# A graph layer on one core: slot products set between the steps of the edge run

## The reference, cut to what matters

```python
h = jnp.maximum(_layernorm(x, axis=-1), 0.0)
m = h[src] + edge_attr
aggr = jax.ops.segment_sum(m, dst, num_segments=N_NODES)
hidden = jax.nn.relu(aggr @ W1 + b1)
mlp_out = hidden @ W2 + b2
return x + (1.0 + eps[0]) * h + mlp_out
```

## Time and profile before

| | us |
|---|---|
| median of 3 runs (545.75 to 546.79) | 546.37 |
| span of the profiled execution | 559.3 |
| PE busy | 493.2 (88%) |
| DVE busy | 486.6 (87%) |
| ACT busy | 418.4 (75%) |
| POOL busy | 337.2 (60%) |

### The profile page before, as it was taken

One profiled execution on the slowest core, in us unless ns is written; L12 is line 12 of the kernel. 1 busy time (PEld: TensorE's weight loads), 2 busy tenths in 40 slices (PEclk: granted clock), 3 DMA queues, 4 the chain that ended last, 5 costly groups with the idle time before them and its releaser, 6 DMA issues.

```text
span 559.3 us, 23317 instructions
## 1 busy us (share of the span) xinstructions
PE 493.2 (88%) x9560; PEld 462.1 (83%) x9560; DVE 486.6 (87%) x712; ACT 418.4 (75%) x637; POOL 337.2 (60%) x200
## 2 busy tenths in 40 slices
PE   0436899999989999999999899999998999999995
PEld 0325799999878888889999798899887998999994
DVE  7996999999997978898999789899896889999960
ACT  0798778888776867868888578788774788788771
POOL 1310003888888888888888888888888878000000
PEclk9999999999999999999999999999998999999998
DMA  7689988988889979999989789998876779667000
GB/s 193 237 283 279 273 268 263 280 219 222 206 226 244 268 205 249 246 276 228 241 212 235 169 206 259 300 225 235 219 199 154 207 207 239 187 203 214 16 10 19
DMA packets 99110, 120.58 MB, mean 216 GB/s; under 512 B 71160, under 2 KB 72792, under 8 KB 98870
## 3 DMA queue, kind: packets, MB, share of 16 engines
q1 hardware_dynamic: 74854, 108.13, 64.0%
q0 software_dynamic: 24144, 10.89, 15.1%
HBM read 112.50 MB, written 6.48 MB: 213 GB/s over the span
## 4 chain that ended last, share of the span: by engine, by line
PE 78%; ACT 8%; DVE 7%; issue 5%; DMA 1%; SPq 0%; DVEq 0%; ACTq 0%
PE agg_ps L1021 29%; PE oct_ps L1009 22%; PE agg_ps L1015 16%; PE key_ps L1033 5%; PE mlp_ps L1038 4%; ACT gathered_edges L894 3%; ACT adj L858 2%; DVE lo_hot L561 2%; DVE z L561 2%; PE key_ps L1026 1%; DMA gathered_edges<-in_dst 1%; ACT hid L871 1%; DVE hl L591 0%; DVE hot L568 0%; ACT hl L882 0%
## 5 line engine op out<-in xcount | busy, mean ns | idle before, releaser
L858 ACT ACTIVATE adj<-oct_ps 128x784 f16<-128x784 f32 x360 | 299.0, 865 | 108.6 <-PE oct_ps L1009 90.9
L490 POOL DMA_INDIRECT gathered_edges<-h_rows,gather_src x160 | 301.3, 1883 | 48.8 <-issue 48.8
L1021 PE MATMUL agg_ps<-hl,adj 128*128 128x192 f16 x2205 | 234.1, 246 | 2.0 <-issue 1.5
L561 DVE TENSOR_TENSOR lo_hot<-iota_z,key 128x2048 f16<-128x2048 f16 x180 | 219.3, 1218 | 0.0
L1009 PE MATMUL oct_ps<-z,lo_hot 128*128 128x98 f16 x2880 | 192.4, 209 | 17.7 <-DVE lo_hot L561 6.5
L561 DVE TENSOR_TENSOR z<-z_marks,key 128x1568 f16<-128x1568 f16 x180 | 174.3, 969 | 12.7 <-PE oct_ps L1009 7.0
L1009 PEld LDWEIGHTS oct_ps<-z,lo_hot 128*128 128x128 f16 x2880 | 165.3, 100 | 22.6 <-issue 11.2
L1021 PEld LDWEIGHTS agg_ps<-hl,adj 128*128 128x128 f16 x2205 | 174.2, 98 | 4.9 <-issue 2.9
L1015 PE MATMUL agg_ps<-edges,hot 128*32 128x96 f32 x3600 | 98.8, 252 | 16.4 <-issue 13.9
L1015 PEld LDWEIGHTS agg_ps<-edges,hot 128*32 128x32 f32 x3600 | 81.2, 111 | 29.9 <-issue 20.7
L461 POOL DMA_INDIRECT win<-packed_keys,row_i x23 | 30.3, 1317 | 74.7 <-DMA gathered_edges<-in_edge_attr 61.2
(11 more groups left out here) (126 smaller groups left out, 182.5 us busy)
## 6 DMA issues: line engine op xcount, KB each, us to landing
edges<-in_edge_attr SPq DMA_DIRECT2D x180, 480.0 KB
gathered_edges<-in_edge_attr SPq DMA_DIRECT2D x16, 480.0 KB
dst<-in_dst SPq DMA_DIRECT2D x180, 5.0 KB
gathered_edges<-h_rows,gather_src POOLq DMA_INDIRECT x160
out<-ob SPq DMA_DIRECT2D x45, 48.0 KB
packed_keys<-adj SPq DMA_DIRECT2D x1, 1632.0 KB, 6.8
h_rows<-gathered_edges SPq DMA_DIRECT2D x1, 1200.0 KB, 9.2
h_rows<-gathered_edges SPq DMA_DIRECT2D x1, 1152.0 KB, 9.0
```

The source lines that it names most:

```text
L490: nc.gpsimd.indirect_dma_start(out=gathered[k][:, g, t, :], out_offset=None, in_=h_dram, in_offset=bass.IndirectOffsetOnAxis(ap=gather_src ...
L561: return nc.vector.tensor_tensor(out.rearrange("p t (w two) -> p t w two", two=2), marks[0:out.shape[0], 0:width].rearrange("p (o w two) - ...
L858: return nc.scalar.activation(adj[k][:, :, 2 * OCT * o:2 * OCT * (o + 1)].rearrange("p h (t q) -> p t h q", q=2), oct_ps[:, o % 2, :].rear ...
L1021: last = nc.tensor.matmul(agg_ps[buf][:, 0:2 * C], adj[buf][:, h, :], hl[:, h, :], start=False, stop=(h == NT - 1), skip_group_check=True)
```

## The change

Three edits. `SLOTS_AFTER` becomes (8, 4, 10, 3, 7, 6, 3, 8) from (10, 2, 0, 6, 10, 8, 4, 9). From block 2 on, 9 of the 10 slot products that now belong to octet 2 are issued inside the edge run, one after each of its first nine steps; the tenth follows the projection. And in the count of passes that a rarely used general path would need, one operation on `need` covers two values where it covered one.

```diff
-SLOTS_AFTER = (10, 2, 0, 6, 10, 8, 4, 9)
+SLOTS_AFTER = (8, 4, 10, 3, 7, 6, 3, 8)
...
-                chain(nc.vector.tensor_scalar(need[:, 0:1], need[:, 0:1], 1.0, 1.0, ALU.add, ALU.max))
+                chain(nc.vector.tensor_scalar(need[:, 0:2], need[:, 0:2], 1.0, 1.0, ALU.add, ALU.max))
...
-            def sum_edges(rows, hots, sums, fresh):
+            def sum_edges(rows, hots, sums, fresh, slots=None):
                 for t in range(GT):
                     for g in range(GROUPS):
                         last = nc.tensor.matmul(sums[GROUP * g:GROUP * (g + 1), :], hots[:, g * GT + t, :], rows[:, g, t, :],
                                                 start=fresh and t == 0, stop=False, skip_group_check=True)
+                    if slots is not None and t < GT - 1:
+                        sum_slots(slots[0], slots[1] + t, slots[1] + t + 1)
                 return last
...
-                        sum_edges(edge_rows(b), hot[b % 2], agg_ps[b % 2][:, 0:C], here is None).then_inc(edges_done, 1)
+                        sum_edges(edge_rows(b), hot[b % 2], agg_ps[b % 2][:, 0:C], here is None,
+                                  ((b - 1) % 2, SLOT_CUTS[o]) if b >= 2 else None).then_inc(edges_done, 1)
...
-                        last = sum_slots((b - 1) % 2, SLOT_CUTS[o], SLOT_CUTS[o + 1])
+                        mixed = GT - 1 if b >= 2 and o == EDGES_AFTER else 0
+                        last = sum_slots((b - 1) % 2, SLOT_CUTS[o] + mixed, SLOT_CUTS[o + 1])
```

## The result

| | before | after |
|---|---|---|
| median, us | 546.58 (545.75 to 551.32, 4 runs) | 645.25 (640.01 to 646.20, 4 runs) |
| span of the profiled execution, us | 559.3 | 643.1 |

The changed kernel takes 1.182 times as long, with a 95% interval of 1.176 to 1.188. Where some executions of a kernel lie over 1.5% above its fastest, the ratios and their intervals leave these out, and the medians do not.

The account below looks back on a forecast made before the run. PE was taken as the bound after DVE's first five blocks. 559.3 + 88 for passages + 23 for ACT - 27 for stalls gave 643 us profiled; between 643 and 628 as a median, 630 us was taken, range 575 to 650.

Parts of the forecast that it names:

- passages: Edge run: changing between 32 and 128 columns of weights costs 0.227 us extra per mixed slot, 387 in all, +88 us.
- ACT late behind the octets: Octet 3 to the next block's slots: with fewer slot products there PE waits for ACT's reads, +23 us net.
- stalls of the edge run: Idle before weight loads in the edge run, and the half clock after the longest, all go: -27 us.
- profiled span: Whole profiled execution of the changed kernel: 559.3 + 88 + 23 - 27 = 643 us.
- from span to time: Whole kernel: the median was 12.9 us below the profiled span, so 643 or 628 was possible and 630 us was taken.
- the first rival: Edge run: the queue hides the passages, price zero or nearly so, median 541 to 550 us; chance 0.06 of no change or small loss.
- The walk through the reads: Behind octets 3 to 7: PE waits for ACT's reads 0.53 us at octet 7, then 0.17, 0.7 us a block.
- The free queue: Edge run: weight loads run ahead, so passages cost nearly nothing, median 541 to 550 us; chance 0.06 of no change or small loss.
- the faster case: Edge run and octets: free passages and no wait for ACT, only the stalls go, 520 to 535 us; chance 0.09.
- One passage hidden: Edge run: price only 0.09 to 0.13 us, +35 to +50, median 575 to 598 us; chance 0.12.
- The clock: Mixed edge run: clock falls to 1.2 GHz in each block for 3.6 us, +77 us, about 710; chance 0.04.
- list of what lifts a block: PE's block, 10.08 to 11.1 us: four attached gathered edge runs of 1.7 us each, and 20.7 us of edge-run stalls.

Follow-up runs that it names:

- shorter reads: From block 2 on ACT reads only half of each octet: on the changed kernel 620.44 us, on the kernel before as control 540.39 us.
- one_lump: Changed kernel with all nine slot products of the edge run in one lump behind step 4, instead of one after each step: 569.19 us, 1.042 of before.
- narrow_slots: Changed kernel with each of the nine slot products in the edge run cut into four matmuls with 32 columns of weights: 584.89 us, 1.070 of before.
- mixed_old_tail: Changed kernel, nine slot products still mixed in, with table (2, 0, 10, 6, 10, 8, 4, 9): 646.61 us, 1.190 of before.
- unmixed_old_tail: Kernel before with table (2, 0, 10, 6, 10, 8, 4, 9) and no slot product inside the edge run: 560.77 us, 1.032 of before.
- near_slots: Kernel before with two slot products moved from octet 0 to octet 1, no mixing: 545.17 us, 1.002 of before.
- double_run: Kernel before with every edge run done twice in a row: 655.17 us, 1.207 of before.
- before_again: Kernel before, unchanged, run for a second trace: 548.75 us, span 546.9 us.
- The table alone: Kernel before with only the new SLOTS_AFTER table, no slot product inside the edge run: 558.05 us, 1.024 of before.

## Why the prediction came out as it did

630 us were predicted, with 575 to 650 as the range, and 645.25 were measured. The mechanism in the kernel is the one forecast; the step from the profiled span to the time is not borne out. The terms can be set beside the runs:

| term | predicted, us | measured, us |
|---|---|---|
| passages, 387 pairs | +88 (0.227 each) | +94 by the step of 0.491 (0.242 each); 87 between the runs with and without the mixing, whose stalls differ too |
| ACT late behind the octets | +23 net | +19 to +22: waits of octets rise from 5.0 to 27.2; shorter reads give 24.8 back, and 5.7 before |
| stalls of the edge run | -27 from the first trace | by starts from 27 to 4 against the first trace (idle 20.7 to 3.8), from 6 to 4 against the second (8.5 to 3.8) |
| profiled span | 643 | 643.1 |
| from span to time | -13 | +1.9 |

*The passages.* The rows into and out of today's edge run carried over. Out of a step the trace of after has 0.18 from the last edge matmul to the slot, as read; back it has 0.186 where I took 0.176, so a step is 0.49 and not 0.476, 6 us in all. The lump shows that the price goes with the passage, and the narrow slots that it goes with the change between 32 and 128 columns of weights. The weight load of the slot starts 0.17 us after the last edge matmul and together with its own matmul. Whether PE is late because the load is, or the load because PE lets running work end first, these runs don't separate.

The Trainium skill, TensorEngine Tiling, Key Properties, says that a change of tiling mode drains the engine. Both runs agree: 11 us for one pair a block in one_lump, and no such cost in a step of narrow_slots. The Trainium skill, TensorE: Matmul & The Clock Gate, Part 3, has the rule on weight loads pulled ahead of running matmuls, on which the first rival stood. The trace agrees within one width (0.08 us ahead), and no load is pulled ahead over a passage here.

*ACT.* The walk through the reads gave 0.53 us at octet 7 and 0.17 at the next octet 0's slots; the block in the timeline has 0.48 and 0.09 at the second place. The step was right as to this table. Its wording, that the ten slots were taken "from there", was too narrow: mixed_old_tail and unmixed_old_tail show that the eight octets from 3 to the next 2 form one stretch in which ACT reads, and that taking ten of its 49 slots away costs 13 to 15 us wherever they are taken. near_slots, which moves two within the stretch, costs nothing.

*Stalls.* They went as predicted, 3.8 us of idle remain. (The addends given for the term make 26, not 27.) But their size was taken from one execution. The second trace has 8.5 of the 20.7, so against it the gain was 2 to 5 us, not 17 or more.

*From span to time.* This step failed. I took part of the 12.9 us between the first span and the median for something that a run without the profiler saves. In fact every run here takes its span plus 1.8 to 1.9 us, the profiled one too (644.98 and 643.1 for after). The difference was mostly the stalls of that one execution, and double_run shows that timed runs have them. Had I kept 643 and added nothing, the forecast would have been 2 us off; the 13 us taken off are nearly the whole of the miss of 15. That 643 was met to 0.1 us is luck all the same. By starts, the way from the first trace to the trace of after is +94 for the passages, +17 for octets that wait and -24 in the edge runs, with -3 for the rest, where the sum had +88, +23 and -27: errors of a few us each cancel.

*The rivals.* The free queue and the faster case needed a price under 0.03 us; it is 0.242. One passage hidden would have shown 0.34 to 0.38 us a step. The clock did not fall in each block: the granted clock is 1.00 in the block shown above. But it fell once, inside a mixed run. First a row of PE's timeline, then two stretches with the columns of the earlier trace rows:

```profile
224.60 0.36 PE L1015 MATMUL agg_ps<-edges,hot 128*32 128x96 f32 x4 [1.05 <-issue]
...
222.40:225.90 3.50, 2.45 (x47) 1.17 (x37) 2.95 (x3) 1.27 (x1) 2.89 (x3) 1.00 0.45 59
225.90:229.30 3.40, 3.40 (x49) 1.49 (x45) 0.00 (x0) 0.00 (x0) 2.79 (x3) 0.52 0.17 21
```

PE had stood idle for 1.05 us in one of the stalls that remain, and was busy 2.45 of 3.50 us; then 1.2 GHz was granted for 6.8 us. The prediction had set against this rival that PE stood idle for 2.4 us at one go before the fall in the earlier trace rows. Here less went before one. The five mixed steps at half clock last 0.75 us each. In the half-clock stretches of before_again, fours and slot products follow at 0.160 us. So by an estimate from these few steps a pair of passages costs 0.27 us, hardly more than at full clock, while the streaming takes twice as long.

*What the sum leaves out.* On usual runs it gives 545 + 94 + 22 = 661, and 645 were measured. The distances between PE's starts, summed by what follows what, show where the 16 us are. From the span of the second trace of before, 546.9, to that of after, 643.1, are +96:

| from the second trace of before to after | us |
|---|---|
| passages | +94 |
| octets waiting for ACT | +22 |
| stalls in the edge runs | -2 |
| ahead of the turned sum | -10 |
| the gathered edge runs and the wait for their DMA | -4 |
| all else | -4 |

So in a usual run of before PE also waits ahead of the turned sum, for DVE's join (5.4 us in the row of before_again, 0.9 in after) and without a cause shown (3.4 us of idle before its loads), and once for the gathered edges (2.6). A PE that is late by its passages or by ACT finds these ready. The table alone shows it too: by starts its octets wait 22 us more than in the second trace, 8 come back ahead of the turned sum and 4 at the gathered runs, and its span is 10.5 us longer. near_slots, a kernel as fast as before, has the wait for DVE's join as well (4.4 us). This is read from single traces, and no run isolates it. The prediction's list of what lifts a block from 10.08 to 11.1 us is short by the same kind of wait: its parts make some 31 of 44 us.

## What to carry to other kernels

Before matmuls of two weight widths are interleaved on TensorE, read what one change of width costs today, at both borders of the run, and multiply it by the number of changes; the own time of the moved work tells nothing. Work that hides a second engine's reads is not free to be moved, even if it is put where it costs its engine nothing. And a profiled execution should be set beside the spread of the timed ones before its stalls are booked as a gain: take the difference between its time and the median off the stalls, not off everything, or take a second trace first.

## What the runs showed of the hardware

A change between matmuls with 32 and with 128 columns of weights, at 2.4 GHz, takes 0.12 us on the way to 128 columns and 0.10 on the way back beyond the streaming (0.178 against 0.0625 from start to start, and 0.186 against 0.083); a pair with the slower start of the next fours is 0.242 us. Over such a change no weight load starts ahead of its matmul; within one width it starts 0.08 us ahead. Four 32-column matmuls in float16 with 192 columns of data fit between float32 steps at 0.083 us, with no such cost. I had not expected that PE's stalls of about 0.6 us without a visible cause would differ from 34 to 8 between two executions of the same program, nor that one idle of 1.05 us in a mixed run would be followed by 6.8 us at 1.2 GHz. What causes the stalls stays open.
